# The first feed-forward's down products in the second layer's input stage: two exact parts, one pass each, and the stage as streams per pair of tiles

## The chip, the cores and the metric

The kernel runs on one core of a Trainium2 chip. The metric is the device time of one execution in microseconds (us), of which the median over several runs is taken.

## The reference

Two transformer blocks on x of B=2, T=512, D=256 in float32. Each adds an attention and a feed-forward of the same normalized input to x:

```python
xn = _layernorm(x, axis=-1)
x = x + _L0_attn_ref(xn, ...) + _L0_ffn_ref(xn, ...)
xn = _layernorm(x, axis=-1)
x = x + _L1_attn_ref(xn, ...) + _L1_ffn_ref(xn, ...)
```

The attention of layer 0 is a chunked gated delta rule over 16 key heads and 32 value heads. Its feed-forward, whose last product this case is about, is

```python
wq_gu = ternary_quant(w_gate_up)
gate, up = jnp.split(jnp.einsum('bsd,hd->bsh', x, wq_gu), 2, axis=-1)
h = jax.nn.silu(gate) * up          # 1024 hidden channels
hn = rms_norm(h)
return jnp.einsum('bsh,dh->bsd', hn, ternary_quant(w_proj))
```

Layer 1 has a grouped-query attention with a root-mean-square norm and rotary tables (16 query, 4 key heads of 16), a mixture of 8 experts, and a feed-forward with weights of -1, 0 and 1, a gelu, and biases.

## The kernel before

The 1024 tokens are 8 tiles of 128 (TT), or 4 pairs (QT). The stages follow one another, with a barrier of all engines between them (`stage_end`): `gdn` (L385, all of layer 0), `layer1_in` (L1502, the input stage of layer 1), `attention` (L1729) and `experts` (L1919).

`gdn` is one program of streams: each part of each engine is a generator that yields the time at which its next piece is due, by the tables START, AT and FINAL, and `in_order` (L85) writes an engine's pieces in the order of those times. Its last streams make layer 0's feed-forward: `pe_forward` (L1333) multiplies 16 groups of hidden channels; ACT and DVE form h and POOL sums its squares. Then follow on PE 8 sums over the channels (L1357) and 64 down products 128x256 in float32 (L1367), on DVE the mean (L1433), on POOL its power -1/2 (L1416), and on DVE the addition to the residual stream `yacc`, scaled by that root (L1439). Down products accumulate 8 groups of channels for each tile:

```python
ins = pe.matmul(bank[i][:, u * D:(u + 1) * D], hidden(8 * b + f)[:, t * P:(t + 1) * P],
                down_f[f // 4][:, f % 4, :], start=(f == 0), stop=(f == 7))
```

Between them PE turns the last four tiles of layer 1's ternary weights: DVE compares (`v_second`, L1279 and L1284), PE transposes (`pe_second`, L1300), ACT copies out of PSUM (L1309) and issues the write to memory (L1312 to `up1_d`, L1314 to `down1_d`); `layer1_in` loads them back as w1T and w2T (L1528, L1529). DVE may write a tile of `Yq` only when PE has turned the one before.

`layer1_in` is written out by hand. DVE takes the statistics of all 8 tiles (L1538, L1542, L1545), POOL the root (L1671), DVE the normalized tiles l_xn (L1548). PE transposes each (L1493) and multiplies it with the query, key and value weights (L1646), two tiles at a time; DVE applies the rotary tables (L1559 to L1565), ACT copies three bfloat16 parts of the result (L1602) with subtractions on DVE between them (L1570), and the values (L1594). POOL also clears `vp` and `ks` (L1669, L1676), scales the weights (L1675), forms r, cos_r and sin_r (L1679 to L1687), splits xT exactly into x_hi and x_lo (L1691, L1694), and copies the key parts (L1706). When that split is done, PE multiplies 16 groups of hidden channels of layer 1's feed-forward (L1635) and ACT applies the gelu (L1623); last come the transposed keys (L1663, L1612).

## Time and profile before

| | |
|---|---|
| runs, us | 1602.49, 1596.72, 1597.46 |
| median, us | 1597.46 |
| the profiled execution: its own time, us | 1600.64 |
| its span, us | 1598.7 |
| its mean granted TensorE clock | 0.956 |
| PE busy, us | 1421.7 (89%) |
| DVE busy, us | 1050.9 (66%) |
| ACT busy, us | 850.6 (53%) |
| POOL busy, us | 533.6 (33%) |

Times of the profile are counted from the start of the span and belong to this one execution. An engine's busy time is what its instructions cover; PE is the matrix engine, DVE the vector, ACT the scalar, POOL the general-purpose engine, SP issues transfers. A granted clock of 1.00 is 2.4 GHz, a half of it the lower level.

### The profile page before, as it was taken

What the parts mean: (1) busy time and instruction counts of PE and PEld (TensorE: products, weight loads), DVE (VectorE), ACT (ScalarE), POOL (GpSimd) and SP (SyncE); (2) the same over time, 40 slices, a digit from 0 to 9 for tenths busy, and PEclk for the clock granted to TensorE, in tenths of its full rate; (3) what the DMA queues carried; (4) which work ended last, traced back from release to release, by engine and by line L of the source; (5) the groups of instructions that cost most, each with busy time, mean ns of one, the idle gap of its engine ahead of it and who ended that gap; (6) DMA issues with size and microseconds to landing.
All of it is one profiled execution on the core that took longest, in us unless ns stands there. A gap on an engine that the chain in (4) does not pass through costs nothing. (4 is left out here: it accounts for less than half of the span.)

```text
span 1598.7 us, 35680 instructions
## 1 busy us (share of the span) xinstructions
PE 1421.7 (89%) x13996; PEld 1048.5 (66%) x13996; DVE 1050.9 (66%) x2150; ACT 850.6 (53%) x1728; POOL 533.6 (33%) x562
## 2 busy tenths in 40 slices
...
DMA packets 142485, 56.39 MB, mean 35 GB/s; under 512 B 109776, under 2 KB 134992, under 8 KB 142064
## 3 DMA queue, kind: packets, MB, share of 16 engines
q1 hardware_dynamic: 133424, 48.20, 13.1%
...
## 5 line engine op out<-in xcount | busy, mean ns | idle before, releaser
L1147 POOL TENSOR_TENSOR og<-og,sz 128x256 f32<-128x256 f32 x128 | 93.4, 730 | 524.2 <-DVE og L1090 297.6
L937 DVE SCALAR_TENSOR_TENSOR Yv<-banks,cwall,Yv 128x511 f32<-128x511 f32 (+2 forms) x192 | 131.0, 739 | 3.8 <-ACT Yv L777 3.8
L684 PE MATMUL banks<-wz,xT 128*128 128x256 f32 x512 | 126.3, 390 | 8.0 <-DVE yacc L1110 8.0
L755 PE MATMUL banks<-wo,oT 128*128 128x256 f32 x512 | 128.3, 395 | 1.3 <-ACT oT L929 1.3
L540 PE MATMUL banks<-wv,xT 128*128 128x512 f32 x256 | 120.2, 604 | 3.6 <-DVE Yv L937 3.6
L540 PE MATMUL banks<-wqk,xT 128*128 128x512 f32 x256 | 122.9, 616 | 0.2 <-DVE Yk L937 0.2
L684 PEld LDWEIGHTS banks<-wz,xT 128*128 128x128 f32 x512 | 96.2, 194 | 28.5 <-issue 15.9
L924 ACT ACTIVATE junk<-og 128x512 f32<-128x512 f32 x64 | 40.4, 631 | 140.1 <-POOL og L1147 140.1
L1154 POOL TENSOR_TENSOR rn<-ss,c_half 128x4 f32<-128x4 f32 x64 | 64.5, 1009 | 148.7 <-DVE ss L1104 148.3
L755 PEld LDWEIGHTS banks<-wo,oT 128*128 128x128 f32 x512 | 97.4, 198 | 20.7 <-issue 6.2
L728 PE MATMUL banks<-V,A 128*128 128x128 f32 x512 | 84.2, 287 | 15.8 <-ACT V L904 15.6
L1110 DVE TENSOR_TENSOR yacc<-yacc,banks 128x512 f32<-128x512 f32 x64 | 43.7, 683 | 78.4 <-PE banks L755 77.7
L728 PEld LDWEIGHTS banks<-V,A 128*128 128x128 f32 x512 | 72.7, 191 | 32.8 <-ACT V L904 27.1
L1864 DVE TENSOR_REDUCE mx<-banks 128x1 f32<-128x128 f32 (+3 forms) x128 | 58.5, 489 | 54.5 <-PE banks L1787 52.1
L540 PEld LDWEIGHTS banks<-wv,xT 128*128 128x128 f32 x256 | 46.4, 195 | 45.5 <-issue 45.3
L540 PEld LDWEIGHTS banks<-wqk,xT 128*128 128x128 f32 x256 | 47.0, 198 | 42.9 <-issue 42.6
L1119 POOL TENSOR_TENSOR E<-E,nsk 128x1024 f32<-128x1024 f32 x32 | 60.1, 1898 | 39.9 <-DVE nsk L964 39.0
L777 ACT ACTIVATE Yv<-banks,cwall 128x512 f32<-128x512 f32 x64 | 42.2, 681 | 51.1 <-PE banks L540 51.1
L937 DVE SCALAR_TENSOR_TENSOR Yk<-banks,cwall,Yk 128x511 f32<-128x511 f32 (+2 forms) x96 | 64.4, 739 | 7.1 <-ACT Yk L777 7.1
L1158 POOL TENSOR_TENSOR og<-og,rn 128x512 f32<-128x512 f32 x64 | 66.6, 1041 | 5.0
L1031 DVE COPY_PREDICATED Td<-c_lo,banks 128x512 f32<-128x512 int32 x16 | 11.8, 735 | 84.7 <-PE banks L595 84.7
L1069 DVE SCALAR_TENSOR_TENSOR R<-banks,tab,vn 128x128 f32<-128x128 f32 x192 | 58.4, 346 | 11.3 <-PE banks L697 6.7
...
## 6 DMA issues: line engine op xcount, KB each, us to landing
...
wqk<-in_L_attn_W_qkvz SPq DMA_DIRECT2D x8, 512.0 KB, 4.8
wv<-in_L_attn_W_qkvz SPq DMA_DIRECT2D x8, 512.0 KB, 5.5
...
blk<-cm_d SPq DMA_DIRECT2D x128, 16.0 KB, 1.8
...
Td<-t_d SPq DMA_DIRECT2D x128, 16.0 KB, 1.9
```

What stands on the lines that cost most here:

```text
L540: ins = pe.matmul(bank[b][:, :], xT[:, d, b * S + of_batch, :], w[:, d, :], start=(d == 0), stop=(d == KD - 1))
L684: ins = pe.matmul(bank[7][:, b * 256:(b + 1) * 256], xT[:, d, b * S + q, :], wz[:, d, :], start=(d == 0), stop=(d == KD - 1))
L728: ins = pe.matmul(pK[:, h * DH:(h + 1) * DH], A[k % 2][:, h, n, :], V0[b][:, h, :], start=True, stop=True)
L755: ins = pe.matmul(bank[7][:, b * D:(b + 1) * D], oT[:, b, h, :], wo[k % 2][:, h, :], start=(h == 0), stop=(h == VR - 1))
L937: v.scalar_tensor_tensor(y, bank[b][:, 0:T - j], conv_w(k, t)[:, 3 - j:4 - j], y, ALU.mult, ALU.add).then_inc(s["tap"].sem, 1)
L1069: ins = v.scalar_tensor_tensor(R[b][:, h, :], pK[:, h * DH:(h + 1) * DH], tab[:, k, NEG_EG, h, n:n + 1], vn[k % 2][:, n, h, :], ALU.mult, ...
L1110: v.tensor_tensor(ya, ya, bank[7][:, :].rearrange("p (b d) -> p b d", b=B), ALU.add).then_inc(s["y"].sem, 1)
L1119: pool.tensor_tensor(E[:, h, :, :], E[:, h, :, :], nsk[:, h, :].unsqueeze(2).to_broadcast([P, NT, P]), ALU.mult).then_inc(s["nE"].sem, 1)
L1147: pool.tensor_tensor(og[:, n, :, :], og[:, n, :, :], sz[q % 2][:, b, :].rearrange("p (h d) -> p h d", h=VR), ALU.mult).then_inc(s["osz"].s ...
L1154: pool.tensor_tensor(rn[:, q, :, :], ss[:, q, :, :], c["neghalf"][:, 0:B * VR].rearrange("p (b h) -> p b h", b=B), ALU.pow).then_inc(s["rn ...
L1158: pool.tensor_tensor(o, o, rn[:, q, :, :].unsqueeze(3).to_broadcast([P, B, VR, DH]), ALU.mult).then_inc(s["ogn"].sem, 1)
L1864: v.tensor_reduce(x[:, t, g:g + 1], top[i % 2][:, 0:(t + 1) * P], AX, ALU.max).then_inc(s["mx"].sem, 1)
```

## The change

The down products leave `gdn` and become the first work of `layer1_in`. ACT rounds each of the 16 groups of h to float32r (`act_high`), DVE subtracts 12 and POOL 4 of them from h (`v_low`, `pool_low`), so that high and low part add up to h exactly, and PE multiplies both with the ternary weights, which float32r holds exactly (`pe_down0`): 128 products of one pass where 64 of float32 stood. Sums, mean and root move along (`pe_squares`, `v_mean`, `pool_root`).

The stage is rewritten as streams per pair of tiles, ordered by a table of due times, LIN. Statistics, root, l_xn, r, x_hi, x_lo and the rotary tables are made per pair (`v_pair`, `pool_pair`, `pool_x_parts`); the first layer-1 hidden group needs the first two pairs instead of all four. The memset of `qs` moves from POOL to DVE (`v_zero`). All of the stage's 22 loads are issued by SP; 9 of them were ACT's. In `gdn`, tiles of SBUF are placed in another order, the hidden groups get one array, and SP waits at the end for the down weights.

```diff
-    down_f = [line(t).rearrange("p (f d) -> p f d", d=D) for t in (wv, sq)]
-    hid = [line(t) for t in (E, CM, A[0], vn[0])]
+    down_r = rounded("f0_down", "wv", [P, FF // P, D])
+    assert [base[n] - base["E"] for n in ("CM", "A0", "vn0")] == [8192, 16384, 24576] and base["sq"] - base["wv"] == 4096 and base["Td"] - base["t512"] == 2048
+    f0h = nc.alloc_sbuf_tensor_at("f0_h", [P, 2 * FF // P, 512], F32, offset=base["E"])
+    f0sums = nc.alloc_sbuf_tensor_at("f0_acc", [P, B, 512], F32, offset=base["t512"])
+    m["f0"] = f0h, rounded("f0_lo", "E", [P, 2 * FF // P, 512]), f0sums, down_r
     f0hs, f0sq = ([line(Yv)[:, (2 * i + u) * 512:(2 * i + u + 1) * 512] for u in range(2)] for i in range(2))
-    f0acc = [t512[:, :], line(Td)]
-    hidden = lambda n: hid[n // 4][:, n % 4 * 512:(n % 4 + 1) * 512]
+    f0acc = [f0sums[:, b, :] for b in range(B)]
+    hidden = lambda n: f0h[:, n, :]
     in_groups = lambda t: t.rearrange("p (g e) -> p g e", e=GR64)
     over_group = lambda t, g: t[:, g % 2, :].unsqueeze(2).to_broadcast([P, 16, GR64])
...
-        sp.dma_start(down_f[1], m["down_d"][:, 4:8, :]).then_inc(s["f0w2"].sem, 16)
+        sp.dma_start(down_r[:, 4:8, :].bitcast(F32), m["down_d"][:, 4:8, :]).then_inc(s["f0w2"].sem, 16)
         sp.wait_ge(*s["proj"](7, LAST))
-        sp.dma_start(down_f[0], m["down_d"][:, 0:4, :]).then_inc(s["f0w2"].sem, 16)
+        sp.dma_start(down_r[:, 0:4, :].bitcast(F32), m["down_d"][:, 0:4, :]).then_inc(s["f0w2"].sem, 16)
+        sp.wait_ge(*s["f0w2"]())
...
-        yield START["f0"] + FSTEP * 16
-        pe.wait_ge(*s["f0h"]())
-        pe.wait_ge(*s["f0acc"]())
-        for t in range(TT):
-            ins = pe.matmul(bank[2][:, t:t + 1], f0acc[t // QT][:, t % QT * P:(t % QT + 1) * P], c["ones"][:, 0:1], start=True, stop=True)
-        ins.then_inc(s["f0ss"].sem, 1)
-        pe.wait_ge(*s["f0w2"]())
-        for i in range(4):
-            yield START["f0"] + FSTEP * (17 + i)
-            if i == 2:
-                pe.wait_ge(*s["f0ms"]())
-            for u in range(2):
-                b, t = divmod(2 * i + u, QT)
-                for f in range(8):
-                    ins = pe.matmul(bank[i][:, u * D:(u + 1) * D], hidden(8 * b + f)[:, t * P:(t + 1) * P], down_f[f // 4][:, f % 4, :], start=(f == 0), stop=(f == 7))
-            ins.then_inc(s["f0dn"].sem, 1)
...
-        yield START["f0"] + FSTEP * 18
-        pool.wait_ge(*s["f0ms"]())
-        pool.tensor_tensor(rt[:, :], rt[:, :], c["neghalf"][:, 0:TT], ALU.pow).then_inc(s["f0r"].sem, 1)
...
-        yield START["f0"] + FSTEP * 17
-        v.wait_ge(*s["f0ss"]())
-        v.tensor_scalar(rt[:, :], bank[2][:, 0:TT], 1.0 / FF, float(np.finfo(np.float32).eps), ALU.mult, ALU.add).then_inc(s["f0ms"].sem, 1)
-        yield START["f0y"]
-        v.wait_ge(*s["f0r"]())
-        v.wait_ge(*s["y"](3, LAST))
-        for t in range(TT):
-            v.wait_ge(*s["f0dn"](t // 2))
-            v.scalar_tensor_tensor(yacc[:, t, :], bank[t // 2][:, t % 2 * D:(t % 2 + 1) * D], rt[:, t:t + 1], yacc[:, t, :], ALU.mult, ALU.add).then_inc(s["f0y"].sem, 1)
...
+LIN = {
+    "lo13": 17.2, "lo14": 17.6, "lp15": 11.6, "ss": 0.4, "ms": 15.6, "root": 10.4, "vz": 0, "kz": 21.2, "ones": 43.2, "qz": 64.8, "dn0": 11.2, "dn1": 18.8, "dn2": 22, "dn3": 22.8, "y0": 20,
...
+}
...
+    hidden, h_lo, squares, down = m["f0"]
+    h_hi = nc.alloc_sbuf_tensor_at("f0_hi", [P, 2 * FF // P, 512], F32R, offset=m["h1_at"])
+    by_pool = [n for n in range(16) if n % 4 == 3]
+    by_vector = [n for n in range(16) if n % 4 != 3]
+    lo_made = lambda n: s["flp"](by_pool.index(n)) if n in by_pool else s["flo"](by_vector.index(n))
...
+        for t, name, landed in ((an, "attn_norm_w", s["l1an"]), (mn, "moe_norm_w", s["l1s"])):
+            for k in range(KD):
+                sp.dma_start(t[:, k:k + 1], a["L1_attn_" + name][k * P:(k + 1) * P].rearrange("(p o) -> p o", o=1)).then_inc(landed.sem, 16)
+            if t is an:
+                sp.dma_start(cos[:, :, :], a["rope_cos"].rearrange("(q p) e -> p q e", p=P)).then_inc(s["l1s"].sem, 16)
+                sp.dma_start(sin[:, :, :], a["rope_sin"].rearrange("(q p) e -> p q e", p=P)).then_inc(s["l1s"].sem, 16)
+        sp.dma_start(b2[:, :], a["L1_ffn_b2"].partition_broadcast(P)).then_inc(s["l1s"].sem, 16)
         sp.dma_start(w1T[:, :, :].bitcast(F32), m["up1_d"]).then_inc(s["f1w"].sem, 16)
         sp.dma_start(w2T[:, :, :].bitcast(F32), m["down1_d"]).then_inc(s["f1w"].sem, 16)
...
+    def act_high(act):
+        for n in range(16):
+            yield LIN[f"hi{n}"]
+            act.copy(h_hi[:, n, :], hidden[:, n, :]).then_inc(s["fhi"].sem, 1)
+
+    def v_low(v):
+        for j, n in enumerate(by_vector):
+            yield LIN[f"lo{n}"]
+            v.wait_ge(*s["fhi"](n))
+            v.tensor_tensor(h_lo[:, n, :], hidden[:, n, :], h_hi[:, n, :].bitcast(F32), ALU.subtract).then_inc(s["flo"].sem, 1)
+
+    def pool_low(pool):
+        for j, n in enumerate(by_pool):
+            yield LIN[f"lp{n}"]
+            pool.wait_ge(*s["fhi"](n))
+            pool.tensor_tensor(h_lo[:, n, :], hidden[:, n, :], h_hi[:, n, :].bitcast(F32), ALU.subtract).then_inc(s["flp"].sem, 1)
...
+    def pe_squares(pe):
+        yield LIN["ss"]
         for t in range(TT):
+            ins = pe.matmul(bank[0][:, t:t + 1], squares[:, t // QT, t % QT * P:(t % QT + 1) * P], c["ones"][:, 0:1], start=True, stop=True)
+        ins.then_inc(s["fss"].sem, 1)
+
+    def v_mean(v):
+        yield LIN["ms"]
+        v.wait_ge(*s["fss"]())
+        v.tensor_scalar(rt[:, :], bank[0][:, 0:TT], 1.0 / FF, float(np.finfo(np.float32).eps), ALU.mult, ALU.add).then_inc(s["fms"].sem, 1)
+
+    def pool_root(pool):
+        yield LIN["root"]
+        pool.wait_ge(*s["fms"]())
+        pool.tensor_tensor(rt[:, :], rt[:, :], c["neghalf"][:, 0:TT], ALU.pow).then_inc(s["fr"].sem, 1)
+
+    def pe_down0(pe, i):
+        b = i // 2
+        yield LIN[f"dn{i}"]
+        if i >= 2:
+            pe.wait_ge(*s["fy"](2 * (i - 2) + 1))
+        for u in range(2):
+            t = (2 * i + u) % QT
+            for part in (h_hi, h_lo):
+                for f in range(8):
+                    n = 8 * b + f
+                    if i % 2 == 0 and u == 0:
+                        pe.wait_ge(*(s["fhi"](n) if part is h_hi else lo_made(n)))
+                    elif u == f == 0 and part is h_hi:
+                        pe.wait_ge(*lo_made(8 * b + 6))
+                        pe.wait_ge(*lo_made(8 * b + 7))
+                    ins = pe.matmul(bank[6 + i % 2][:, u * D:(u + 1) * D], part[:, n, t * P:(t + 1) * P], down[:, f, :], start=(part is h_hi and f == 0), stop=(part is h_lo and f == 7))
+        ins.then_inc(s["fdn"].sem, 1)
...
+    def v_pair(v, i):
+        yield LIN[f"y{i}"]
+        if i == 0:
+            v.wait_ge(*s["fr"]())
+        v.wait_ge(*s["fdn"](i))
+        for u in range(2):
+            t = 2 * i + u
+            v.scalar_tensor_tensor(xa[:, t, :], bank[6 + i % 2][:, u * D:(u + 1) * D], rt[:, t:t + 1], xa[:, t, :], ALU.mult, ALU.add).then_inc(s["fy"].sem, 1)
+        yield after(i, "st")
+        v.wait_ge(*s["fy"](2 * i + 1))
+        for t in range(2 * i, 2 * i + 2):
             ins = v.bn_stats(bn[:, t, :], xa[:, t, :])
         ins.then_inc(s["st"].sem, 1)
-        v.wait_ge(*s["st"]())
-        for t in range(TT):
+        v.wait_ge(*s["st"](i))
+        for t in range(2 * i, 2 * i + 2):
...
+        v.wait_ge(*s["ag"](i))
+        v.tensor_scalar(rs[:, two(i)], mv[:, two(i), 1], LN_EPS, None, ALU.add).then_inc(s["va"].sem, 1)
+        yield after(i, "xn")
+        v.wait_ge(*s["rs"](i))
+        for t in range(2 * i, 2 * i + 2):
             v.tensor_scalar(xn[:, t, :], xa[:, t, :], mv[:, t, 0:1], rs[:, t:t + 1], ALU.subtract, ALU.mult).then_inc(s["x"].sem, 1)
-        v.tensor_tensor(r8[:, :], mv[:, :, 1], rs[:, 0:TT], ALU.mult).then_inc(s["ms"].sem, 1)
-        v.wait_ge(*s["ms"](0))
-        v.tensor_tensor(r8[:, :], r8[:, :], rs[:, 0:TT], ALU.mult).then_inc(s["ms"].sem, 1)
+        v.tensor_tensor(r8[:, two(i)], mv[:, two(i), 1], rs[:, two(i)], ALU.mult).then_inc(s["ms"].sem, 1)
+        v.wait_ge(*s["ms"](2 * i))
+        v.tensor_tensor(r8[:, two(i)], r8[:, two(i)], rs[:, two(i)], ALU.mult).then_inc(s["ms"].sem, 1)
+
+    def pool_pair(pool, i):
+        yield after(i, "rs")
+        pool.wait_ge(*s["va"](i))
+        pool.tensor_tensor(rs[:, two(i)], rs[:, two(i)], c["neghalf"][:, 0:2], ALU.pow).then_inc(s["rs"].sem, 1)
+        yield after(i, "r8")
+        pool.wait_ge(*s["ms"](2 * i + 1))
+        pool.tensor_scalar(r8[:, two(i)], r8[:, two(i)], LN_EPS, None, ALU.add).then_inc(s["r8e"].sem, 1)
+        pool.wait_ge(*s["r8e"](i))
+        pool.tensor_tensor(r8[:, two(i)], r8[:, two(i)], c["neghalf"][:, 0:2], ALU.pow).then_inc(s["r"].sem, 1)
+        yield after(i, "cs")
+        pool.wait_ge(*s["r"](i))
+        if i == 0:
+            pool.wait_ge(*s["l1s"]())
+        of_token, rows = r8[:, two(i)].unsqueeze(2).to_broadcast([P, 2, HD // 2]), slice(2 * i % QT, 2 * i % QT + 2)
+        pool.tensor_tensor(csr[:, two(i), :], cos[:, rows, :], of_token, ALU.mult)
+        pool.tensor_tensor(snr[:, two(i), :], sin[:, rows, :], of_token, ALU.mult).then_inc(s["rot"].sem, 1)
...
+    def pe_turned_x(pe, i):
+        yield after(i, "xT")
+        if i == 0:
+            pe.wait_ge(*s["fms"]())
+        for t in range(2 * i, 2 * i + 2):
+            pe.wait_ge(*s["x"](t))
+            pe_turned(pe, s, "xTt", c, bank, xn, t, "xTe")
...
+    def pool_x_parts(pool, i):
+        yield after(i, "xhi")
+        pool.wait_ge(*s["xTe"](2 * i + 1))
+        pool.tensor_copy(x_part[0][:, :, two(i), :], xT[:, :, two(i), :]).then_inc(s["xhi"].sem, 1)
+        yield after(i, "xlo")
+        pool.wait_ge(*s["xhi"](i))
+        pool.tensor_tensor(x_part[1][:, :, two(i), :], xT[:, :, two(i), :], x_part[0][:, :, two(i), :].bitcast(F32), ALU.subtract).then_inc(s["xlo"].sem, 1)
...
+        yield LIN["qz"]
+        v.memset(qs[:, :, :, :], 0.0).then_inc(s["qz"].sem, 1)
...
+        if i == 0:
+            pool.wait_ge(*s["slots"](1))
+        pool.wait_ge(*s["part2"](i))
+        for j, part in enumerate(K_PARTS):
+            ins = pool.tensor_copy(ks[:, two(i), :, j * HD:(j + 1) * HD], parts[:, part, two(i), D:QK * HD].rearrange("p t (g e) -> p t g e", g=KVH))
...
+    def pool_set(pool):
+        yield LIN["vz"]
         pool.memset(vp[:, :, :, :], 0.0).then_inc(s["slots"].sem, 1)
+        yield LIN["kz"]
+        pool.memset(ks[:, :, :, :], 0.0).then_inc(s["slots"].sem, 1)
         for k in range(KD):
+            yield LIN[f"wq{k}"]
+            if k == 0:
+                pool.wait_ge(*s["l1w"]())
+                pool.wait_ge(*s["l1an"]())
             pool.tensor_scalar(wqkv[:, k, :], wqkv[:, k, :], an[:, k:k + 1], None, ALU.mult).then_inc(s["wq"].sem, 1)
...
+    def streams(engine, by_pair, others):
+        in_order([(0.0, f(engine, i)) for i in range(QT) for f in by_pair] + [(0.0, f(engine)) for f in others])
+
+    def on_tensor(pe):
+        streams(pe, (pe_down0, pe_turned_x, pe_qkv), (pe_squares, pe_hidden, pe_turned_keys))
+
+    def on_vector(v):
+        streams(v, (v_pair, v_rope), (v_low, v_mean, v_zero))
+
+    def on_scalar(act):
+        streams(act, (act_turned_x, act_values, act_parts), (act_high, act_hidden, act_turned_keys))
+
+    def on_gpsimd(pool):
+        streams(pool, (pool_pair, pool_x_parts, pool_keys), (pool_low, pool_root, pool_set))
```

What the streams make of it is seen in the order of each engine's instructions. PE at the end of `gdn` and the start of `layer1_in`, before (wv and sq hold the down weights, E, CM, A and vn the hidden groups; Yq is a tile of ternary weights):

```order
L1357 MATMUL banks<-c_ones,t 128x1 x4
L1357 MATMUL banks<-c_ones,Td 128x1 x4
L1300 MATMUL banks<-c_identb,Yq 128x128 x8
L1367 MATMUL banks<-wv,E 128x256 x4
L1367 MATMUL banks<-sq,CM 128x256 x4
...
L1300 MATMUL banks<-c_identb,Yq 128x128 x8
```

and in the change, where the last `gdn` row is the first of these:

```order
L1306 MATMUL banks<-c_identb,Yq 128x128 x32
L1566 MATMUL banks<-c_ones,f_acc 128x1 x8
L1594 MATMUL banks<-f_down,f_hi 128x256 x8
L1594 MATMUL banks<-f_down,f_lo 128x256 x8
...
L1470 MATMUL banks<-c_ident,l_xn 128x128 x4
L1594 MATMUL banks<-f_down,f_hi 128x256 x8
```

The four groups of turned weights now follow each other with nothing between. The products of four tiles (pairs 0 and 1) stand ahead of the transposes of pair 0, those of pairs 2 and 3 behind them.

POOL at the start of `layer1_in`, before:

```order
L1669 MEMSET vp 128x1024
L1671 TENSOR_TENSOR rs<-rs,c_half 128x8
L1675 TENSOR_SCALAR wqkv<-wqkv,an 128x384 x2
L1676 MEMSET ks 128x4096
L1679 TENSOR_SCALAR r<-r 128x8
```

and in the change:

```order
L1768 MEMSET vp 128x1024
L1561 TENSOR_TENSOR f_lo<-f_h,f_hi 128x512 x2
L1577 TENSOR_TENSOR f_r<-f_r,c_half 128x8
L1561 TENSOR_TENSOR f_lo<-f_h,f_hi 128x512 x2
L1627 TENSOR_TENSOR rs<-rs,c_half 128x2
L1770 MEMSET ks 128x4096
L1627 TENSOR_TENSOR rs<-rs,c_half 128x2
L1658 CAST x_hi<-xT 128x2x256
L1661 TENSOR_TENSOR x_lo<-xT,x_hi 128x2x256
```

The memset of `ks` follows the root of pair 0 at once; it stood behind the scaled weights. DVE there, in the change (before, 8 additions L1439, 8 L1538, 8 L1542 and 8 l_xn L1548 followed each other):

```order
L1555 TENSOR_TENSOR f_lo<-f_h,f_hi 128x512 x7
L1572 TENSOR_SCALAR f_r<-banks 128x8
L1555 TENSOR_TENSOR f_lo<-f_h,f_hi 128x512 x5
L1604 SCALAR_TENSOR_TENSOR yacc<-banks,f_r,yacc 128x256 x2
L1608 BN_STATS bn<-yacc 128x6 x2
L1612 BN_AGGR mv<-bn 128x2 x2
L1615 TENSOR_SCALAR rs<-mv 128x2
L1619 TENSOR_SCALAR l_xn<-yacc,mv,rs 128x256 x2
```

## Rows read from the trace of the kernel before

**Rows 1.** Busy time by stretch (windows); "x" counts records, then granted clock, DMA share, GB/s.
```profile
1269.00:1286.90 17.90, 15.96 (x86) 13.64 (x84) 4.61 (x9) 2.02 (x2) 0.00 (x0) 1.00 0.22 59
1286.90:1300.00 13.10, 6.83 (x21) 4.22 (x22) 10.59 (x27) 1.81 (x6) 9.25 (x6) 0.61 0.78 225
...
1313.00:1338.00 25.00, 19.00 (x98) 13.10 (x97) 9.76 (x17) 21.92 (x35) 12.43 (x25) 1.00 0.00 0
```

**Rows 2.** Timeline, end of `gdn`: start us, us, engine, line, operation [idle before].
```profile
1253.49 0.84 PE L1300 MATMUL banks<-c_identb,Yq 128*128 128x128 bf16 x8
...
1254.37 1.01 ACT L1309 CAST UB<-banks 128x1024 f32<-128x1024 bf16 x1 [4.19 <-PE banks L1300]
1254.48 1.28 DVE L1284 SCALAR_TENSOR_TENSOR Yq<-UB,q_s,Yq 128x1024 bf16<-128x1024 f32 x1
...
1285.00 0.88 DVE L1439 SCALAR_TENSOR_TENSOR yacc<-banks,f_r,yacc 128x256 f32<-128x256 f32 x2 [6.54 <-PE banks L1367]
...
1286.93 0.95 POOL L1669 MEMSET vp<- 128x1024 f32 x1 [30.97 <-POOLq L63]
```

**Rows 3.** DMA issues of 1240 to 1300: KB each, median us to landing.
```profile
l1w2T<-down_d SPq DMA_DIRECT2D x1, 1024.0 KB, 9.4
...
down_d<-kt ACTq DMA_DIRECT2D x1, 512.0 KB, 3.5
```

**Rows 4.** Timeline, one-pass down products in two parts, in `experts`.
```profile
1501.93 2.05 PE L1960 MATMUL banks<-l1w2T,h_hi 128*128 128x256 f32 x8
...
1508.71 1.12 PE L1960 MATMUL banks<-l1w2T,h_lo 128*128 128x256 f32 x8
```

**Rows 5.** Grouped instructions by form: ACT, DVE and POOL on 128x512 f32.
```profile
L1390 ACT ACTIVATE Yv<-vn 128x512 f32<-128x512 f32 x4 | 2.5, 625 | 2.7 <-DVE vn L1430 2.7
...
L2094 DVE TENSOR_TENSOR cmp<-cmp,before 128x512 f32<-128x512 f32 x1 | 0.7, 692 | 0.0
...
L1413 POOL TENSOR_TENSOR Td<-Td,Yv 128x512 f32<-128x512 f32 x7 | 9.0, 1279 | 9.6 <-ACT Yv L1390 9.6
```

**Rows 6.** Timeline, DVE beside POOL in `layer1_in`.
```profile
1292.31 6.82 DVE L1548 TENSOR_SCALAR l_xn<-yacc,mv,rs 128x256 f32<-128x256 f32 x8 [1.75 <-POOL rs L1671]
...
1295.03 3.65 POOL L1676 MEMSET ks<- 128x4096 bf16 x1
...
1305.39 5.14 POOL L1694 TENSOR_TENSOR x_lo<-xT,x_hi 128x1024 fp32r<-128x1024 f32 x2
...
1305.70 2.63 DVE L1565 TENSOR_TENSOR qk<-ro 128x320 f32<-128x320 f32 x1
...
1310.81 0.48 DVE L1565 TENSOR_TENSOR qk<-ro 128x320 f32<-128x320 f32 x1
```

**Rows 7.** Grouped instructions by form of 1286 to 1340, `layer1_in`.
```profile
L1493 PE MATMUL banks<-c_ident,l_xn 128*128 128x128 f32 x16 | 3.4, 352 | 8.2 <-DVE l_xn L1548 8.1
...
L1675 POOL TENSOR_SCALAR wqkv<-wqkv,an 128x384 f32<-128x384 f32 x2 | 2.8, 1414 | 0.0
...
L1663 PE MATMUL banks<-c_identb,ks 128*128 128x128 bf16 x32 | 2.3, 220 | 1.1 <-ACT kT L1612 1.1
```

**Rows 8.** Timeline of `layer1_in`.
```profile
1286.96 2.71 DVE L1538 BATCH_NORM_STATS2 bn<-yacc 128x6 f32<-128x256 f32 x8 [1.09 <-PEq L63]
...
1290.64 1.64 POOL L1671 TENSOR_TENSOR rs<-rs,c_half 128x8 f32<-128x8 f32 x1 [2.76 <-DVE rs L1545]
...
1295.16 4.26 PE L1646 MATMUL banks<-wqkv,xT 128*128 128x384 f32 x8
...
1310.82 2.82 PE L1646 MATMUL banks<-wqkv,xT 128*128 128x384 f32 x8 [1.26 <-ACT vp L1594]
...
1320.69 0.62 PE L1635 MATMUL banks<-x_lo,l1w1T 128*128 128x512 f32 x2
...
1321.15 0.63 PE L1635 MATMUL banks<-x_hi,l1w1T 128*128 128x512 f32 x2
...
1337.22 0.69 ACT L1623 ACTIVATE h<-banks,b 128x512 f32<-128x512 f32 x1 [0.21 <-PE banks L1635]
```

More of the change, by code:

```diff
@@ L1647, in pe_qkv, with v_rope @@
             ins.then_inc(s["qkv"].sem, 1)
[L1649 to L1658 removed]
+    def v_rope(v, i):
+        yield after(i, "rope")
+        v.wait_ge(*s["qkv"](2 * i + 1))
+        v.wait_ge(*s["rot"](i))
+        if i:
+            v.wait_ge(*s["rope"](i - 1))
+        v.tensor_tensor(ro[0][:, :, :, :], half(i, 0), turns(csr, i), ALU.mult)
+        v.tensor_tensor(ro[1][:, :, :, :], half(i, 1), turns(snr, i), ALU.mult)
+        v.tensor_tensor(ro[2][:, :, :, :], half(i, 0), turns(snr, i), ALU.mult)
+        v.tensor_tensor(ro[3][:, :, :, :], half(i, 1), turns(csr, i), ALU.mult).then_inc(s["ro"].sem, 1)
+        v.wait_ge(*s["ro"](i))
+        v.tensor_tensor(qk[:, two(i), :, 0:HD:2], ro[0][:, :, :, :], ro[1][:, :, :, :], ALU.subtract)
+        v.tensor_tensor(qk[:, two(i), :, 1:HD:2], ro[2][:, :, :, :], ro[3][:, :, :, :], ALU.add).then_inc(s["rope"].sem, 1)
+        for n in range(2):
+            yield after(i, f"sub{n}_")
+            v.wait_ge(*s[f"part{n}"](i))
+            v.tensor_tensor(flat[:, two(i), :], flat[:, two(i), :], parts[:, n, two(i), :], ALU.subtract).then_inc(s[f"sub{n}"].sem, 1)
@@ new lines, in v_zero, with act_values @@
+    def v_zero(v):
+        yield LIN["qz"]
+        v.memset(qs[:, :, :, :], 0.0).then_inc(s["qz"].sem, 1)
+    def act_values(act, i):
+        yield after(i, "vp")
+        if i == 0:
+            act.wait_ge(*s["slots"](0))
+        act.wait_ge(*s["ro"](i))
+        for u in range(2):
+            act.activation(vp[:, 2 * i + u, :, 0:HD], qkv(i)[:, u, QK * HD:QK * HD + KVH * HD].rearrange("p (g e) -> p g e", g=KVH),
+                           ACT.Copy, scale=r8[:, 2 * i + u:2 * i + u + 1]).then_inc(s["vp"].sem, 1)
```

226 lines of the change are left out of this document (77 added, 149 removed), and 14 rows, old and new, of tables (LIN, START).

## The prediction

> **What bounds the kernel now.** I first read the windows from the end of `gdn` on [rows 1]. In the last 17.9 us of `gdn` PE is busy for 15.96 at full granted clock and POOL not at all: PE alone bounds, with the down products. In the first 13.1 us of `layer1_in` PE is busy for 6.83 at granted clock 0.61, while DVE has 10.59 and POOL 9.25: normalization and its square roots bound. From 1313 on PE (19.0 of 25) and ACT (21.9) fill the stage together. Then the timeline of the end of `gdn` [rows 2]: the first group of turned weights is on PE from 1253.49 to 1254.33; behind it 64 down products and three more groups run to 1284.96, the last addition ends at 1285.88, and the barrier lets `layer1_in` start at 1286.93. The stage ends with the last gelu at 1337.91 [rows 8]: 51.0 us long.
>
> **A. The end of `gdn`.** Down products, sums of squares, root and additions leave. What remains is a loop of four units: DVE writes a ternary tile, PE turns it, and DVE may write the next one only then. One turn costs 1.28 (L1284) + 0.84 (L1300, measured at low clock) + 2 x 0.04 for the two hand-overs = 2.2 [rows 2]. The other DVE instruction of the unit (L1279) runs beside PE. Unit 1 ends at 1254.33 as before; with three more the transposes end at 1260.9, ACT's cast (1.05) at 1262.0, and the last write to memory lands 3.5 later [rows 3], at 1265.5. The barrier takes the 1.04 it takes now (1285.88 to 1286.93), so the stage begins at 1266.5, **20.4 us earlier**. Bounds: 21.5 without the wait for landing being last in line with ACT, 18.5 if each cast also waits for the write two units before it. SP's new wait for the layer-0 down weights costs nothing: its transfer was needed at 1254 before. The scattered placement of tiles and everything ahead in `gdn` keeps its order on every engine: 0.
>
> **B. `layer1_in` grows.** Four stretches, counted from its start.
>
> *0 to 13.4: splitting.* ACT makes 16 rounded copies (L1549). Nearest price 0.63 each [rows 5], 10 in all, off the path. The remainders are two-input subtractions in SBUF: 12 on DVE at 0.61 to 0.69 (nearest: 0.69 in [rows 5]; 0.61 by scaling a 128x320 one of 0.48 [rows 6] to 512 columns without its start) = 7.3, and 4 on POOL at 1.28 = 5.1 [rows 5]. Whether they run together is the open price. The timeline [rows 6] shows the pair: DVE's L1565, two SBUF inputs, lasts 0.48 alone and 2.63 beside POOL's subtraction L1694, as long as one of the two POOL instructions (5.14/2). So they take turns: 7.3 + 5.1, plus 0.95 for POOL's memset ahead, 13.4. If nothing is held, DVE's 7.3 and POOL's 6.1 run side by side and PE comes last, at about 9. The Trainium skill, page "Advanced Engine Details and Errata", disagrees with itself: the note under VectorE Performance Modes, Mode Summary, has GpSimd interfere with two-port vector instructions only, and the table under Instruction Support gives tensor_tensor no such mode, so by it the stretch would be about 9; the line under GPSIMD Details adds instructions with two SBUF inputs, so by it the stretch is 13.4. The 2.63 in the row is for the second. PE's share here is small: a one-pass product 128x256 takes 0.12 (1.12 for 8 with the last one's latency) once the clock is up, 0.23 while it is low [rows 4]; the 64 of pairs 0 and 1 run behind the splits, done at 13.2.
>
> *13.4 to 20.4: the first pair.* Two additions 0.9 [rows 2], two bn_stats at 0.34 to 0.41 [rows 8] and small ones, 2.2 together; the root for 2 columns, 0.7 (1.64 is for 8 [rows 8]; bounds 0.3 and 1.6): 16.3. Behind the root stands POOL's `memset ks`, 3.65, and DVE's l_xn wants to start at the same moment. By [rows 6] eight l_xn last 6.82, of which one spans the memset; the rest are at 0.4 to 0.6. So the first l_xn ends at 20.4. PE cannot use the time: the transposes of pair 0 are ahead of the down products of pairs 2 and 3 in its queue, as the order shows.
>
> *20.4 to 29.9: pairs 2 and 3.* PE: 64 x 0.12 = 7.7, the transposes 0.7, 0.6 for a low clock after the pause: 29.4. POOL beside: two roots, x_hi 0.5, x_lo 1.3, the root and tables of r 1.4, and wqkv 2.8 [rows 7], together 7.4 with 2 more of hand-overs: about 29.9, when the first qkv product can run.
>
> *29.9 to 65: the old PE work.* qkv 16 x 0.64 = 10.2 (2.82 for four with the last one's latency, [rows 8]), hidden 64 x 0.232 = 14.9 (a pair starts 0.46 after the other, [rows 8]), the other transposes about 3.2 (two thirds of what [rows 7] show as busy, since those hold each short group's latency): 28.3. Before, 42.7 us passed from the first qkv (1295.16) to the end, so 14.4 were waits and low clock: for l_xn behind the memset, for x_hi and x_lo, for gelu. The streams put hidden groups between the qkv pairs, and x_hi and x_lo come per pair; I keep half, 7 (bounds 4 and 11). The stage is 29.9 + 28.3 + 7 = **65, 14 longer**.
>
> The down products themselves cost PE some 28 before (1254.33 to 1284.96 less three groups of transposes, [rows 2]) and 128 x 0.12 = 15.4 now. The 12 saved there and 5 or so saved on waits behind the barrier are mostly given back to the splits and the memset, which have nothing else to cover them.
>
> The 9 transfers that move from ACT's queue to SP's: ACT is free of issuing them, and cos, sin and b land ahead of the big weight loads; the first hidden group wants those 30 us after the start. The slowest of the stage's loads took 9.4 [rows 3]: 0. `memset qs`, 2048 columns more on DVE at the end, is behind its last subtraction: 0, at worst 1.
>
> **Sum.** -20.4 + 14 = -6.4. On the profiled execution's own 1600.64 that is 1594.2; that execution stands 3.2 over the median of the runs, 1597.46, so the forecast is **1591.1**.
>
> **Rivals.**
> 1. *The memset passes by l_xn.* L_xn is granted SBUF first, or the two do not meet. For: in [rows 6] they met in mid-stream, here both become free on the same event. Against: POOL needs no hand-over to go on, DVE does. 3.5 less: 1587.6. Chance 0.22.
> 2. *The splits do not hold each other.* Against it the 2.63 of [rows 6]. The first stretch ends at 9: 4.2 less, 1586.9; together with rival 1, 1583.4. Chance 0.10.
> 3. *The streams wait in each other's queues.* A gelu waiting on ACT keeps a copy of xT behind it, a hidden group on PE keeps a qkv behind it: 11 us of waits in place of 7, 1595. For: one table sets four engines' order, and each wait now stands before several others' work. Against: the barriers between steps are finer. Chance 0.17.
> 4. *Slower: TensorE stays at its lower level, 1.2 GHz.* By [rows 8] four qkv take 4.26 at that level, 2.82 at the higher, and the granted clock was 0.61 from 1286.9 to 1300 [rows 1], where PE was lightly used; the eight products of [rows 4] took 2.05 after a light stretch, 1.12 later. If the streams leave PE in short bursts, every us of its work at 1.2 GHz costs one more. It decides once over 6.4 us are lost, about a quarter of the last stretch; at half of it 14 are: 1605.3, slower. Against: PE has 28 of 35 us there to do. Chance 0.09.
>
> My forecast keeps 0.42. **Range**: 1584 to 1599; it leaves out part of rival 2 below and most of rival 4 above, and holds the bounds of A (2 us) and of the waits (3 to 4). The forecast's own range is 1588.5 to 1594.5. A measurement of this kernel tells about 0.5%, 8 us, from no change: "faster" is below 1589.5, a fifth of the forecast's own chance (0.08) and most of rivals 1 and 2 (0.30): 0.38. "Slower" is above 1605.4: 0.05. The same: 0.57.
>
> **What would show it.** The profile of the changed kernel should have the stage's start near 1266.5; DVE's remainders alternating with POOL's, each held one 1.3 us or more; the first l_xn lasting about 4 us; PE idle for 4 to 6 us ahead of the first transposes; 8 down products in 0.96; the first qkv near 30 us into the stage, its end near 65. I am wrong in A if the stage begins after 1269; in B's first half if remainders on DVE last 0.6 throughout; in its second if PE's granted clock is under 0.9 from the first qkv on, or its waits are over 11 us.

## The result and the profile after

The changed kernel takes 1595.38 us (median of 20 runs, 1589.73 to 1601.70), the one before 1602.52 (median of 20, 1593.50 to 1610.23). The ratio is 0.9958, with a 95% interval of 0.9940 to 0.9976: 6.7 us faster by the ratio, 0.42% (7.1 between the two medians), outside the noise and inside the half per cent that the prediction called the same. The forecast was 6.4 us less, and 1591.1 as a time. The time came out 4.3 higher because the forecast stood on the median of three runs, 1597.46, and that of twenty is 1602.52; the difference of the two kernels is what can be compared. The profiled execution of the change took 1592.58 us, with a span of 1590.8 and a mean granted clock of 0.945.

In this text the **tail** is the time from the end of the first group of turned weights to the memset of `vp` with which `layer1_in` begins, and the **stage** the time from there to the first copy of `qs` (POOL L1752; L1844 in the changed kernel), with which `attention` begins. Both kernels have these marks. Before, the tail was 32.6 (1254.33 to 1286.93) and the stage 51.5; after, they are 13.1 and 63.8: 7.2 us less in sum.

The end of `gdn` in the timeline of the changed kernel; these rows answer to [rows 2]:

```profile
1248.48 1.01 ACT L1315 CAST UB<-banks 128x1024 f32<-128x1024 bf16 x1 [4.34 <-PE banks L1306]
1248.55 1.28 DVE L1290 SCALAR_TENSOR_TENSOR Yq<-UB,q_s,Yq 128x1024 bf16<-128x1024 f32 x1 [0.41 <-PE banks L1306]
...
1254.87 1.04 PE L1306 MATMUL banks<-c_identb,Yq 128*128 128x128 bf16 x8 [1.45 <-DVE Yq L1290]
...
1255.94 1.01 ACT L1315 CAST kt<-banks 128x1024 f32<-128x1024 bf16 x1 [1.47 <-PE banks L1306]
1256.98 0.52 ACTq L1320 DMA_DIRECT2D down_d<-kt  x1
...
1261.51 0.95 POOL L1768 MEMSET vp<- 128x1024 f32 x1 [16.03 <-POOLq L63]
```

The loop of DVE and PE is what bounds it: each waits for the other (0.41 on DVE, 1.45 on PE, in the brackets). A turn, from one group of transposes to the next, takes 2.49 where 2.2 was forecast. PE has nothing else to do here, the granted clock from 1248.44 to 1261.51 is 0.50, the lower level, and a group of transposes stays at 1.04, against 0.61 among the down products before.

The stage, in the order in which the prediction goes through it, with the rows that answer to [rows 6] and [rows 8]:

```profile
1261.52 8.42 ACT L1549 CAST f_hi<-f_h 128x512 fp32r<-128x512 f32 x16 [4.57 <-PEq L63]
1261.55 3.54 PE L1566 MATMUL banks<-c_ones,f_acc 128*128 128x1 f32 x16 [5.65 <-PEq L63]
...
1262.17 1.90 DVE L1555 TENSOR_TENSOR f_lo<-f_h,f_hi 128x512 fp32r<-128x512 f32 x3 [7.36 <-ACT f_hi L1549]
...
1264.25 4.39 DVE L1555 TENSOR_TENSOR f_lo<-f_h,f_hi 128x512 fp32r<-128x512 f32 x4 [0.18 <-ACT f_hi L1549]
...
1264.96 2.05 PE L1594 MATMUL banks<-f_down,f_hi 128*128 128x256 f32 x8
...
1268.65 4.19 DVE L1555 TENSOR_TENSOR f_lo<-f_h,f_hi 128x512 fp32r<-128x512 f32 x5
...
1270.40 1.26 PE L1594 MATMUL banks<-f_down,f_lo 128*128 128x256 f32 x8
1270.80 3.19 POOL L1561 TENSOR_TENSOR f_lo<-f_h,f_hi 128x512 fp32r<-128x512 f32 x2
...
1272.76 0.86 DVE L1604 SCALAR_TENSOR_TENSOR yacc<-banks,f_r,yacc 128x256 f32<-128x256 f32 x2
...
1275.63 3.51 POOL L1770 MEMSET ks<- 128x4096 bf16 x1
1275.71 3.89 DVE L1619 TENSOR_SCALAR l_xn<-yacc,mv,rs 128x256 f32<-128x256 f32 x2 [0.81 <-POOL rs L1627]
1279.43 1.09 PE L1470 MATMUL banks<-c_ident,l_xn 128*128 128x128 f32 x4 [3.93 <-DVE l_xn L1619]
...
1280.17 2.06 PE L1594 MATMUL banks<-f_down,f_hi 128*128 128x256 f32 x8
...
1290.21 2.75 PE L1671 MATMUL banks<-wqkv,xT 128*128 128x384 f32 x8
...
1322.98 0.62 PE L1757 MATMUL banks<-c_identb,ks 128*128 128x128 bf16 x8 [0.82 <-ACT kT L1764]
```

Three remainders take 1.90 beside the memset of `vp`, four take 4.39 beside POOL's own. The last of the twelve ends at 11.3 into the stage, when the first addition starts. The first pair of l_xn takes 3.89 beside the memset of `ks`; most of PE's 3.93 of idle time comes from it. Then windows of the same kernel: the first 13.5 us of the stage, and the two parts before and behind the first qkv product (columns as in [rows 1]):

```profile
1261.50:1275.00 13.50, 13.45 (x78) 13.38 (x79) 12.44 (x20) 8.42 (x16) 9.23 (x7) 0.66 0.66 199
...
1261.51:1290.21 28.70, 24.73 (x153) 24.48 (x153) 23.41 (x43) 9.18 (x19) 20.44 (x18) 0.72 0.35 103
1290.21:1325.35 35.14, 30.71 (x138) 19.60 (x136) 24.65 (x48) 26.12 (x47) 20.54 (x49) 1.00 0.00 1
```

Behind the first qkv product PE's granted clock is 1.00 and it is busy for 30.7 of 35.1 us. In the first 13.5 us it has no pause either (13.45 busy), at a granted clock of 0.66: the sums of squares take 3.5 of them, and pair 0's products end at 10.2. So if the splits had taken no time at all, the first addition could have come 1.1 us sooner and no more, unless PE's own work got shorter.

### The profile page after: what moved, and what is told of

The parts are those of the page before. It is cut to its first block and busy times, and to the rows that moved or that the text cites. A ratio compares the mean times of both kernels' runs of the same rounds, so it can differ in the third digit from the quotient of the medians.

```text
span 1590.8 us, 35747 instructions
## 1 busy us (share of the span) xinstructions
PE 1415.9 (89%) x13996; PEld 1047.1 (66%) x13996; DVE 1065.1 (67%) x2172; ACT 856.8 (54%) x1744; POOL 538.8 (34%) x582
## 5 line engine op out<-in xcount | busy, mean ns | idle before, releaser
L734 PE MATMUL banks<-V,A 128*128 128x128 f32 x512 | 84.4, 288 | 15.8 <-ACT V L910 15.6
L734 PEld LDWEIGHTS banks<-V,A 128*128 128x128 f32 x512 | 72.7, 191 | 32.8 <-ACT V L910 27.2
L1956 DVE TENSOR_REDUCE mx<-banks 128x1 f32<-128x128 f32 (+3 forms) x128 | 58.3, 488 | 51.5 <-PE banks L1879 49.3
L1075 DVE SCALAR_TENSOR_TENSOR R<-banks,tab,vn 128x128 f32<-128x128 f32 x192 | 58.4, 346 | 11.3 <-PE banks L703 6.7
L1037 DVE COPY_PREDICATED Td<-c_lo,banks 128x512 f32<-128x512 int32 x16 | 11.7, 731 | 80.2 <-PE banks L601 80.2
```

Of the source, the lines that this page charges most:

```text
L734: ins = pe.matmul(pK[:, h * DH:(h + 1) * DH], A[k % 2][:, h, n, :], V0[b][:, h, :], start=True, stop=True)
L1075: ins = v.scalar_tensor_tensor(R[b][:, h, :], pK[:, h * DH:(h + 1) * DH], tab[:, k, NEG_EG, h, n:n + 1], vn[k % 2][:, n, h, :], ALU.mult, ...
L1956: v.tensor_reduce(x[:, t, g:g + 1], top[i % 2][:, 0:(t + 1) * P], AX, ALU.max).then_inc(s["mx"].sem, 1)
```

## The experiments

All are edits of the changed kernel, but for e9. "xT" is the start of the first transposes, "qkv" that of the first qkv product, "y" that of the first addition, each from the start of the stage.

| run | tail | y | xT | qkv | stage | tail + stage |
|---|---|---|---|---|---|---|
| before | 32.6 | | 6.1 | 8.2 | 51.5 | 84.1 |
| e9, before again | 32.2 | | 6.1 | 8.3 | 53.0 | 85.2 |
| the change | 13.1 | 11.3 | 17.9 | 28.7 | 63.8 | 76.9 |
| e1, the change again | 13.1 | 11.2 | 17.9 | 27.7 | 62.7 | 75.8 |
| e2, all remainders on DVE | 13.1 | 12.0 | 18.7 | 29.2 | 64.1 | 77.1 |
| e3, early memset of ks | 13.1 | 11.6 | 15.6 | 24.7 | 59.3 | 72.3 |
| e4, 8 remainders on POOL | 13.1 | 11.7 | 19.7 | 29.8 | 64.6 | 77.7 |
| e5, float32 down products | 13.1 | 12.8 | 19.5 | 34.2 | 69.0 | 82.1 |
| e6, nine loads on ACT | 13.1 | 18.3 | 25.0 | 36.0 | 70.8 | 83.9 |
| e7, pair 2 ahead of transposes | 13.1 | 11.3 | 17.9 | 27.2 | 61.7 | 74.8 |
| e8, late wait for weights | 10.5 | 11.3 | 17.9 | 28.7 | 63.7 | 74.2 |
| e10, e3 and e8 | 10.5 | 11.6 | 15.5 | 24.6 | 59.3 | 69.8 |
| e11, e10, pair 2, weights | 10.5 | 11.4 | 17.3 | 22.1 | 59.3 | 69.8 |

Each row is one profiled execution. e2 to e9 were timed only once (1592.87 to 1605.17), which tells nothing at differences of this size; they are read by the marks.

**e1 and e9: what repeats.** Both kernels as they are, for second profiles.

> The changed kernel once more, for a second profile. Stage means from the start of the vp memset to the first copy of the attention stage (63.8 us in the first profile, 51.5 before the change); tail means from the end of the first group of turned weights to the start of that memset (13.1, before 32.6). Theory: both repeat within 0.7 us, while the part ahead of the tail and the attention and experts stages, which the change leaves alone, differ between executions by several us (they stood 5.9 us early and 5.2 us long in the first profile). Rival: those two shifts belong to the change (placement of tiles, a lower granted clock after the new stage) and repeat as well.

> The kernel before the change, for a second profile. Theory: the tail of the first stage (from the end of the first turned group to the memset of vp) and the stage repeat within 0.7 us at 32.6 and 51.5, so tail and stage together are 84.1 against 75.8 to 76.9 in the two profiles of the change; all else that differed between those profiles is spread of executions. Rival: tail and stage spread by several us as the rest does, and the difference of the two kernels cannot be read there.

The ratio of e1 was 0.9962 (0.9936 to 0.9988). Tail and stage sum to 76.9 and 75.8 with the change, 84.1 and 85.2 without: 8.3 us less in the mean. The 0.7 us that were expected were too narrow for the stage, which spread by 1.2 and 1.5. In the second profile of the change the first qkv product came 1.0 sooner, at a granted clock of 0.81 ahead of it in place of 0.72. Everything else moves far more: the first turned group ended at 1248.44 in the first profile of the change and 1253.09 in the second, at 1254.33 and 1251.50 in those of before, and at up to 1261.63 in e8, whose order of work there is the same; `attention` and `experts` took 265.5, then 255.7 us. So the 5.9 us that `gdn` was early and the 5.2 us that the last stages were long in the first profile belong to the executions. The rival that the change itself made these two shifts falls. A shift of one or two us ahead of the tail is not excluded by so few profiles: tail and stage give 8.3 and the runs 6.7.

**e2 and e4: who makes the remainders.**

```diff
-    by_pool = [n for n in range(16) if n % 4 == 3]
-    by_vector = [n for n in range(16) if n % 4 != 3]
+    by_pool = []
+    by_vector = list(range(16))
```

> All 16 remainders on DVE, none on POOL. Theory (DVE's two-input subtractions and POOL's hold each other): each takes 0.68, 16 of them 10.9, so the additions of pair 0 start 11.7 us into the stage where they started at 11.3 with four on POOL, and the stage stays at 63.8, within 1. Rival (they run together): DVE's 12 would have ended at 8.9 and the four added ones lengthen the stage by 2.8, to 66.6.

e4 has `n % 2` and `n % 2 == 0` in these two lines.

> Eight remainders on POOL in place of four, eight on DVE. Theory (turns): 8 x 0.68 and 8 x 1.3 to 1.4 end at about 16.9 with the root of the feed-forward on POOL between them, the root of pair 0 is behind POOL's last one, and the stage is 3 to 4.5 longer, 67 to 68. Rival (they run together): POOL ends at 0.95 + 10.2 + 2.0 = 13.2, when the variance of pair 0 comes, and the stage changes by less than 1.

e2's stage was 64.1, as the theory had it, not 66.6. How it came there was not as expected, so the agreement to 0.3 is partly luck:

```profile
1269.58 5.51 DVE L1556 TENSOR_TENSOR f_lo<-f_h,f_hi 128x512 fp32r<-128x512 f32 x9 [7.36 <-ACT f_hi L1550]
...
1275.08 4.29 DVE L1556 TENSOR_TENSOR f_lo<-f_h,f_hi 128x512 fp32r<-128x512 f32 x7
1275.24 5.64 POOL L1578 TENSOR_TENSOR f_r<-f_r,c_half 128x8 f32<-128x8 f32 x1 [5.37 <-DVE f_r L1573]
1280.91 0.88 DVE L1605 SCALAR_TENSOR_TENSOR yacc<-banks,f_r,yacc 128x256 f32<-128x256 f32 x2 [1.54 <-POOL f_r L1578]
```

The sixteen were done at 10.5, 0.9 earlier than the twelve beside POOL: that alone excludes that the two engines subtract without holding each other. But POOL's root, 2.03 in the change, lasted 5.64, to 1.5 behind DVE's last remainder. So the first addition waited for the root and started at 12.0. That the root waited for all seven of DVE's subtractions is a reading and not shown: in the change it took 2.03 although four of them followed each other beside it just as closely (their starts 0.60 apart in both), and 2.03 beside three in e4 (the 1.89 below).

e4 fell between the two. Its remainders took turns, but the stage grew by 0.8 to 1.9 only, not 3 to 4.5:

```profile
1273.53 6.33 POOL L1562 TENSOR_TENSOR f_lo<-f_h,f_hi 128x512 fp32r<-128x512 f32 x4 [0.27 <-ACT f_hi L1550]
1274.00 6.41 DVE L1556 TENSOR_TENSOR f_lo<-f_h,f_hi 128x512 fp32r<-128x512 f32 x4 [0.35 <-ACT f_hi L1550]
...
1280.41 1.89 DVE L1556 TENSOR_TENSOR f_lo<-f_h,f_hi 128x512 fp32r<-128x512 f32 x3
...
1282.57 5.01 POOL L1562 TENSOR_TENSOR f_lo<-f_h,f_hi 128x512 fp32r<-128x512 f32 x4
...
1284.02 0.87 DVE L1605 SCALAR_TENSOR_TENSOR yacc<-banks,f_r,yacc 128x256 f32<-128x256 f32 x2 [1.72 <-PE banks L1595]
...
1287.54 0.70 POOL L1628 TENSOR_TENSOR rs<-rs,c_half 128x2 f32<-128x2 f32 x1
```

Four on each engine take 6.4 us together, 1.6 a pair, where the two durations alone are 0.61 and 1.28. DVE's other three (1.89) ran beside POOL's root and were not held. POOL's last four (5.01, 1.25 each) began when DVE had made all of its own; they had DVE's additions out of PSUM and its statistics beside them and were held by neither. Only the root of pair 0 waited behind them, for some 1.2 us, and the first addition waited for PE (1.72), not for a remainder. So the engines do take turns where both subtract, at a little less than the sum of the two; the expectation summed all sixteen durations, and only four pairs met.

The Trainium skill, page "SBUF — State Buffer", section "SBUF: two separate sides", calls the port pair that the two engines share an exclusive lock, taken for a whole instruction by a DVE instruction in a two-port mode, or by one with two SBUF inputs only against a GpSimd one that reads SBUF. The traces agree: subtraction against subtraction is held (6.41 for four), subtraction against memset is not (1.90 for three), l_xn against memset is (3.89).

**e3: the memset of ks at the start.**

```diff
-    "kz": 21.2,
+    "kz": 0.1,
```

> The memset of ks right behind that of vp, at the stage's start, in place of behind the first root; nothing else moves. Theory: it held the first l_xn for 3.2 us and PE, whose queue has pairs 2 and 3 behind it, for 3.9; a memset does not hold the two-input subtractions (three took 1.90 beside the vp memset), so the first l_xn ends at 14.7 in place of 17.9 and the stage is 3 shorter, 60.8. Rival A: the end is set by the PE and ACT work after the first qkv product and the stage changes by less than 1. Rival B: the memset holds the subtractions as it held l_xn, the splits end 3.5 later and nothing is won, 63.8.

```profile
1272.07 3.51 POOL L1770 MEMSET ks<- 128x4096 bf16 x1
1273.92 1.90 DVE L1555 TENSOR_TENSOR f_lo<-f_h,f_hi 128x512 fp32r<-128x512 f32 x3 [0.18 <-ACT f_hi L1549]
...
1285.76 0.73 DVE L1619 TENSOR_SCALAR l_xn<-yacc,mv,rs 128x256 f32<-128x256 f32 x2 [0.81 <-POOL rs L1627]
...
1295.91 2.85 PE L1671 MATMUL banks<-wqkv,xT 128*128 128x384 f32 x8 [0.38 <-POOL wqkv L1776]
```

The remainders beside the memset are not held (1.90 for three), l_xn is back at 0.73 for two, and the stage is 59.3, 3.4 to 4.6 under the two profiles of the change, where 3 was expected. The theory holds; both rivals fall. The forecast's rival 1, that the memset would pass by l_xn, is priced by this run: 4 us where 3.5 were worked out. The first qkv product now waits for POOL's scaled weights.

**e5: the two-part form undone.** The products take the hidden groups in float32; the rounding copies and the remainders go.

```diff
-            for part in (h_hi, h_lo):
+            for part in (hidden,):
...
-                    ins = pe.matmul(..., part[:, n, t * P:(t + 1) * P], down[:, f, :], ...)
+                    ins = pe.matmul(..., part[:, n, t * P:(t + 1) * P], down[:, f, :].bitcast(F32), start=(f == 0), stop=(f == 7))
```

> The down products of the new stage as 64 in float32 straight from the hidden groups, with no rounding copies and no remainders; place and streams as in the change. Theory: the two-part form saves 12 us of PE (64 x 0.43 = 27.7 against 128 x 0.12 = 15.4), but its splits hold the first pair back; without them the additions start at about 9 and the first l_xn ends at 15.3 in place of 17.9, PE has no pause, and the first qkv product comes at 32 in place of 28: the stage is 3 to 4 longer, 67. Rival A: PE's 12 us count in full, 75. Rival B: the splits cost more than they bring, under 62.

```profile
1265.02 3.54 PE L1566 MATMUL banks<-c_ones,f_acc 128*128 128x1 f32 x16 [5.65 <-PEq L63]
1268.42 16.16 PE L1589 MATMUL banks<-f_down,f_h 128*128 128x256 f32 x64
...
1284.96 13.98 PE L1589 MATMUL banks<-f_down,f_h 128*128 128x256 f32 x64
```

The stage was 69.0, 5.2 to 6.3 longer. PE's products take 30.1 in place of the 20 of the change (from 1264.96 to 1275.5 and from 1280.17 to 1289.9); of these 10 us the stage loses 5 to 6, since some 4 go into the pause that PE had for l_xn. It is now busy for all of the 34.2 us up to the first qkv product. I had expected the first addition at 9: the 8 sums of squares alone take 3.5 at the start of the stage, and pair 0's products begin at the lower clock (granted 0.78 from 1268.5 to 1277.8), so it came at 12.8, later than with the splits. The memset of ks still held l_xn behind it.

**e6: the nine loads back on ACT's queue**, ahead of its copies.

```diff
     def on_scalar(act):
+        for t, name, landed in ((an, "attn_norm_w", s["l1an"]), (mn, "moe_norm_w", s["l1s"])):
+            for k in range(KD):
+                act.dma_start(...)
...
         streams(act, ...)
```

> The nine loads of the stage that moved to SP's queue issued by ACT again, ahead of its rounding copies. What the prediction had: 0 for the move. Theory now: ACT's copies are the first link of the stage's chain, nine issues take ACT 6.8 us (before the change from 1286.93 to 1293.7), so every later step comes that much later less the 0.5 that DVE and POOL catch up: stage 69 to 70. Rival: the chain of DVE and POOL absorbs it, since DVE is held for 3 us anyway: 66 to 67, or nothing, 63.5.

```profile
1272.71 0.91 ACTq L1790 DMA_DIRECT2D an<-in_L_attn_attn_norm_w  x2
...
1276.86 2.11 ACTq L1795 DMA_DIRECT2D gw<-in_L_attn_gate_w  x1
1278.99 0.75 ACTq L1796 DMA_DIRECT2D l_wo<-in_L_attn_w_o  x1
1279.79 2.70 ACT L1540 CAST f_hi<-f_h 128x512 fp32r<-128x512 f32 x5 [11.64 <-issue]
```

ACT's first copy starts 7.1 us into the stage, the first addition comes 7.1 later, at 18.3, and the stage is 70.8: none of it is absorbed. The move of the loads is worth 7 to 8 us, as much as the whole change brings.

**e7: pair 2 ahead of the transposes of pair 0** in PE's order.

```diff
-    "dn2": 22,
+    "dn2": 19.0,
```

> PE's down products of pair 2 ahead of the transposes of pair 0 in its queue; the memset of ks stays where it is. Theory: PE is idle for 3.9 us behind the held l_xn and can do these 32 products (3.85) there; after that POOL's list up to the scaled weights ends at 27.1 and becomes the bound of the first qkv product (27.7 to 28.7 now), so the stage is 1 to 2 shorter, 61.5 to 62.5. Rival A: it is 3.9 shorter, PE being the only bound. Rival B: nothing, since PE's pause was covered.

```profile
1289.86 0.66 PE L1470 MATMUL banks<-c_ident,l_xn 128*128 128x128 f32 x4 [1.24 <-DVE l_xn L1619]
...
1299.09 2.85 PE L1671 MATMUL banks<-wqkv,xT 128*128 128x384 f32 x8 [1.95 <-POOL wqkv L1776]
```

The stage was 61.7 (1.0 to 2.1 shorter). PE did pair 2's products in its pause, and the first qkv product then waited 1.95 us for POOL's scaled weights, at 27.2, where 27.1 was expected. That the queue order keeps PE from work, and that POOL is the bound next, is shown.

**e8: the barrier without the last landings.** The last two writes get semaphores of their own; SP waits for them before it loads w2T, ACT before the copies that reuse their tiles.

```diff
-                act.dma_start(m["down1_d"]..., raw1[g - 6]...).then_inc(out.sem, 16)
+                act.dma_start(m["down1_d"]..., raw1[g - 6]...).then_inc(late[g - 8].sem, 16)
...
+        sp.wait_ge(*s["late0"]())
+        sp.wait_ge(*s["late1"]())
         sp.dma_start(w2T[:, :, :].bitcast(F32), m["down1_d"]).then_inc(s["f1w"].sem, 16)
...
             yield LIN[f"hi{n}"]
+            if n == 0:
+                act.wait_ge(*s["late0"]())
+            if n == 14:
+                act.wait_ge(*s["late1"]())
```

> The barrier at the end of the first stage no longer waits for the last two writes of turned weights; SP waits for them ahead of the load of w2T, ACT ahead of the copies that reuse their tiles. Theory: the 13.1 us from the first turned group to the stage's start are 7.4 of transposes, 1.1 for ACT's cast, 3.5 of landing and 1.0 of barrier; 3 to 3.5 of them go, to 9.6 to 10, and the stage stays at 63. Rival: the barrier waits for something else (SP's loads, ACT's issue) and less than 1 goes, or ACT's first copy waits for the landing instead and the stage grows by what the tail loses.

The tail went from 13.1 to 10.5 and the stage stayed at 63.7. The stage starts 1.9 after ACT's last issue in place of 4.5: 2.6 of the landing's 3.5 were exposed, less than the 3 to 3.5 expected. The rival falls. What fills these 1.9 us is not shown.

**e10 and e11: the parts together.**

> The early memset of ks and the late wait for the turned weights together. Theory: both add, since one shortens the tail (13.1 to 10.5) and the other the stage (62.7 to 63.8 down to 59.3): tail and stage 69.8 in place of 75.8 to 76.9, so some 6.5 us or 0.4% under the changed kernel and 0.8% under the one before, ratio 0.992. Rival: with the stage starting sooner, loads or ACT's waits for the landings stand in its way and less than 4 us of the 6.5 come.

> As e10, and PE's down products of pair 2 ahead of the transposes of pair 0, and POOL's scaled weights taken ahead of and right behind the root of pair 0, where POOL had pauses of 1.2 and 3.5 us. Theory: in e3 the first qkv product waited for the scaled weights at 24.7; now PE sets it: 64 + 64 products and the transposes without a pause, 23 to 24, the stage 58. Rival: the second half of the scaled weights holds l_xn of pair 0 for 1.2 us, and pair 2's products push the transposes back by 3.9, so that what follows on ACT and DVE comes late and the stage is longer, 60 to 62.

e10's time was 1589.43 (median of 12) against 1601.39 before: 0.9938 (0.9906 to 0.9970). Tail and stage are 69.8, so both savings add. e11, which also has the table's `"dn2": 19.0, "wq0": 19.1, "wq1": 21.3`, took 1588.68 (11 runs), 0.9926 (0.9899 to 0.9953). Its first qkv product came 2.5 us earlier than e10's, at 22.1, yet the stage was 59.3 again: PE then waited for the l_xn of pair 2,

```profile
1288.95 2.75 PE L1679 MATMUL banks<-wqkv,xT 128*128 128x384 f32 x8
1293.66 1.05 PE L1471 MATMUL banks<-c_ident,l_xn 128*128 128x128 f32 x4 [1.96 <-DVE l_xn L1627]
...
1296.21 3.46 PE L1679 MATMUL banks<-wqkv,xT 128*128 128x384 f32 x8
```

and the next qkv products ran at the lower clock (3.46 in place of 2.75). The wait and the slower products make 2.7, about the 2.5 gained. The stage is neither the 58 of the theory nor the rival's 60 to 62, though the rival had the kind of loss. Both versions are faster than the kernel before. That they are faster than the change their intervals do not show (0.9962, 0.9938 and 0.9926 overlap); the profiles do, by 6 to 7 us of tail and stage.

## Why the prediction was right, point by point

- **The end of gdn.** Forecast 20.4 less; the tail is 19.5 less (32.6 and 13.1), 19.4 between the means with e1 and e9. The term that was off is the turn of the loop, 2.49 in place of 2.2, three times: the sum had 0.84 for the transposes, and at the lower clock they take 1.04. The forecast's mark, a stage that begins near 1266.5, could not tell: the stages of the changed kernel began at 1261.51 and 1266.15, because `gdn` itself is not repeated that well. The landing was 3.5, as in [rows 3]; e8 shows 2.6 of it exposed.
- **The splits.** Forecast 13.4, measured 11.3. That they take turns was right. The step "7.3 + 5.1, plus 0.95" was mis-sized: the memset held nothing, and POOL's last remainder ran beside DVE's additions out of PSUM and delayed nothing. Where both subtract, a pair costs 1.6 (e4). "PE's share here is small" was wrong: the sum left out PE's sums of squares (3.5) and took the products at the higher clock behind the splits. They ran beside them, and PE was done with pair 0 only 1.1 before DVE. Rival 2's 9 us was out of reach, therefore, even if nothing had been held.
- **The first pair and the memset.** Forecast 7.0, from 13.4 to 20.4; measured 6.7, from 11.3 to 17.9. The hold (3.89 for two l_xn) was as read from [rows 6], and e3 shows what it costs.
- **Pairs 2 and 3.** Forecast 9.5, to 29.9; measured 10.8, to 28.7, and 9.8 in e1. PE's clock was at the lower level for the first 20 or so products after the pause (2.06 for eight at 1280.17, 1.12 for eight from 1284.98 on); the forecast had 0.6 for it. That POOL is next, at 27, is shown by e7.
- **The old PE work.** Forecast 35.2, as 28.3 of work and 7 of waits; measured 35.1 and 35.0, but as 30.7 of busy time and 4.4 of idle time. That the two errors of 2.5 cancel is luck; half of the waits was kept without a row for it. The granted clock of 1.00 in the second window excludes rival 4, and with 4.4 idle rival 3's 11 did not come, although its time, 1595, is the one measured.
- **The loads.** "0" was wrong as a price. The sum took ACT's copies at the start of the stage for granted, and that is so only because the loads had moved: e6 puts them at 7 to 8 us. The error did not show in the sum, which priced the kernel with the move; e6, the change without it, has 83.9 of tail and stage, as much as the kernel before (84.1).
- **The sum.** The stage was forecast 14 longer; it was 12.3, and 11.0 between the means of two profiles each. With 19.5 or 19.4 less in the tail that makes 7.2, or 8.3 by the means, for 6.4 forecast; the runs show 6.7. The mechanisms were right but for PE's share in the first stretch; that the sum is this close is partly luck, since terms were off by 2.1 and 1.3 us in opposite directions. The time itself, 1595.38, lies outside the forecast's own range of 1588.5 to 1594.5 and inside the stated one of 1584 to 1599.
- What the parts are worth is now measured: the down products in two parts 5 to 6 us of stage (e5), the loads 7 to 8 (e6). The two cannot be added up. Without the rounding copies ACT has nothing to do in e5 for the first 19.9 us of the stage, so loads on its queue would probably cost little there, and float32 products with the loads left on ACT would stay near e5's 82.1, an estimate against 84.1 and 85.2 before; that was not run.
